# VectorE's Newton step of the previous unit, placed behind both sums of squares and two rotary products of its slot

## The reference

```python
def l2norm(t):
    return t / jnp.maximum(jnp.linalg.norm(t, axis=-1, keepdims=True), 1e-12)

q = l2norm(q) * qs
k = l2norm(k) * ksc
q = q * cos * scale + rotate_half(q) * sin * scale
k = k * cos * inv + rotate_half(k) * sin * inv
# local_attention: each window attends to itself and the window before
sim = jnp.where(mask, -max, einsum(q, k) * 8.0)
out = einsum(softmax(sim), v)
x = attn_layer(shift_tokens(x), ...) + x
x = ffn_layer(shift_tokens(x), ...) + x
```

## Time and profile before

| what | value |
|---|---|
| device time, median of 3 | 4176.0 us (4174.39 to 4178.6) |
| the profiled execution | 4172.81 us |
| its span, first to last instruction | 4171.0 us |
| PE busy | 3756.9 us (90%) |
| DVE busy | 3466.0 us (83%) |
| ACT busy | 3183.2 us (76%) |
| POOL busy | 2641.4 us (63%) |

### The profile page before, as it was taken

The page is one execution under the profiler, slowest core; times in us unless marked ns, Lnnn a source line. Parts: engine busy times, 40 slices in busy tenths (PEclk is TensorE's granted clock), DMA queues, the critical chain, the costliest instruction groups (busy, mean ns, idle before and its releaser), DMA issues. The chain is left out here.

```text
span 4171.0 us, 167237 instructions
## 1 busy us (share of the span) xinstructions
PE 3756.9 (90%) x66080; PEld 2932.9 (70%) x66080; DVE 3466.0 (83%) x6851; ACT 3183.2 (76%) x10379; POOL 2641.4 (63%) x2482
## 2 busy tenths in 40 slices
PE   8958969999999999999995877999999999999996
PEld 7937947777777777777773546777777777777773
DVE  2242249999999999999984869999999999999994
ACT  4434438888888888888882666888888888888884
POOL 0000027777777777778761647787777877777771
PEclk9978979999999999999997898999999999999997
DMA  1000013333333343333330003333333333333331
GB/s 39 19 1 24 19 50 109 117 102 118 96 109 116 102 121 95 108 116 104 118 91 8 1 22 99 116 101 119 102 104 116 104 117 105 102 119 100 107 118 34
DMA packets 547031, 361.36 MB, mean 87 GB/s; under 512 B 32321, under 2 KB 532817, under 8 KB 546001
## 3 DMA queue, kind: packets, MB, share of 16 engines
q1 hardware_dynamic: 546256, 350.66, 28.1%
HBM read 248.59 MB, written 101.97 MB: 84 GB/s over the span
## 5 line engine op out<-in xcount | busy, mean ns | idle before, releaser
L1278 POOL TENSOR_TENSOR lt_t<-lt_t 128x512 f32<-128x512 f32 x768 | 973.7, 1289 | 567.1 <-DVE lt_t L1112 567.1
L1014 ACT ACTIVATE lt_pb<-lt_pb,lt_mx 128x64 f32<-128x64 f32 x3072 | 1023.4, 345 | 0.0
L1284 POOL TENSOR_TENSOR lt_t<-lt_t,lt_rn 128x512 f32<-128x512 f32 x768 | 811.0, 1077 | 117.3 <-DVE lt_rn L1140 116.0
L49 PE MATMUL ps<-lt_wh,lt_xh 128*128 128x512 f32 (+1 forms) x1536 | 581.7, 379 | 150.1 <-DVE lt_t L1112 88.8
L1014 ACT ACTIVATION_READ_ACCUMULATOR lt_pb<-lt_pb,lt_mx 128x1 f32 x3072 | 609.3, 198 | 0.0
L996 ACT ACTIVATE lt_qkT<-ps 128x512 f32<-128x512 f32 x768 | 459.1, 598 | 196.8 <-PE ps L816 196.8
L1123 DVE TENSOR_REDUCE lt_ss<-lt_sq 128x8 f32<-128x512 f32 x768 | 518.9, 676 | 14.1 <-ACT lt_sq L991 9.9
L1112 DVE TENSOR_TENSOR lt_t<-ps,lt_tab 128x512 f32<-128x512 f32 x768 | 523.1, 682 | 2.9
L1118 DVE TENSOR_TENSOR lt_t<-ps,lt_tab 128x512 f32<-128x512 f32 x768 | 522.1, 680 | 1.9 <-PE ps L816 0.6
L51 PE MATMUL ps<-lt_wh,lt_xl 128*128 128x512 f32 (+1 forms) x1536 | 523.2, 341 | 0.0
L50 PE MATMUL ps<-lt_wl,lt_xh 128*128 128x512 f32 (+1 forms) x1536 | 522.8, 340 | 0.0
(11 more groups left out here) (213 smaller groups left out, 7653.0 us busy)
## 6 DMA issues: line engine op xcount, KB each, us to landing
lt_vw<-v_scratch SPq DMA_DIRECT2D x768, 256.0 KB, 3.8
v_scratch<-lt_vv SPq DMA_DIRECT2D x384, 256.0 KB, 2.1
lt_wraw<-in_lt_wqkv SPq DMA_DIRECT2D x56, 384.0 KB, 5.8
moe_w<-in_moe_w SPq DMA_DIRECT2D x32, 256.0 KB, 2.8
lt_wo<-in_lt_wo SPq DMA_DIRECT2D x48, 128.0 KB, 3.8
lt_w<-in_lt_w SPq DMA_DIRECT2D x12, 341.0 KB, 4.4
lt_w<-in_lt_w SPq DMA_DIRECT2D x12, 192.0 KB, 4.0
lt_gl<-in_lt_qs SPq DMA_DIRECT2D x2, 768.0 KB, 7.5
```

What stands on the lines that cost most here:

```text
L49: nc.tensor.matmul(out, lh, rh, start=start, stop=False)
L1014: ins = nc.scalar.activation(p, p, ACT.Exp, bias=mx[:, par, c:c + 1], accum_out=sm[:, par, c:c + 1])
L1278: nc.gpsimd.tensor_tensor(o, o, t2[:, t, :], ALU.add).then_inc(padd[t], 1)
L1284: nc.gpsimd.tensor_tensor(o, o, rn[:, u[1] % 2, 8 * t:8 * t + 8].unsqueeze(2).to_broadcast([P, 8, DH]), ALU.mult).then_inc(qkd[t], 1)
```

## The change

In VectorE's slot the Newton step of u1 moves from its place behind `maxima` to the place between the second sine product and `floor` of u0. GpSimd's, TensorE's and ScalarE's orders stay.

```diff
                     if u3:
                         maxima(u3)
-                    if u1:
-                        newton(u1)
                     c = chunk(L, s, 17)
                     if c:
                         product(c, 0)
...
                         cosine(u0, 0)
                         lengths(u0, 1)
                         sine(u0, 1)
+                    if u1:
+                        newton(u1)
+                    if u0:
                         floor(u0)
                     if u5 and u5[1] % GJ == GJ - 1:
                         update_x(u5)
```

## The result

Median of the runs side by side: 4129.09 us after (4126.63 to 4134.39) against 4175.19 before (4174.05 to 4178.6), a ratio of 0.989 [0.9873, 0.9907]: 46 us faster. The forecast was 20 us. The profiled execution took 4131.38 us, its span 4129.6.

What follows compares the result with a forecast made beforehand. VectorE and TensorE were both taken to be at their limit, VectorE partly blocked by GpSimd. Ordinary pairs +8, slot-15 pairs -8, layer boundaries -20 gave -20 us: median 4156, own range 4135 to 4175, wide range 4100 to 4210.

Steps and rivals of the forecast that it cites:

- What bounded the kernel: VectorE and TensorE both at their limit; Newton operations held up by GpSimd, 0.76 us a slot, 293 us in all.
- What comes later: rn, hence GpSimd's 5.87 us chain to the weights' transposes: new waits in slots without feed-forward work ahead.
- The other signs: Waits before take_values, lengths, product; GpSimd several hundred us on rn, little on rotary products; VectorE's share down 9 points.
- What goes: TensorE's waits on VectorE in slots 3, 4 and 5 of a pair: about 0.8 us gone.
- the forecast of an ordinary pair: Later transposes and gelus +0.2+0.41+0.14+0.37, vanished waits -0.8: +0.3 us on 64.41, +8 us over 24 pairs.
- The pair with slot 15: Loses more to blocked Newton steps before the change: 0.8 us shorter, ten times, -8 us.
- The pair at a layer's boundary: Newton steps stood behind GpSimd's four 1.8 us operations: -1.8 us, eleven times, -20 us.
- The floor: Directly behind rn, done before GpSimd's scaling starts: cost 0; if it lost, up to 1.0 us of the slot.
- the third rival: Floor operation blocked by GpSimd's scaling, rotary products 1.05 us later: +100 to 120 us, 4270; chance 0.06.
- The feed-forward normalisation: In slot 7, moves up to GpSimd's weight normalisation; both passes can be blocked: 0 to 0.3 us a pair.
- The second rival: GpSimd's chain to the weights' transposes longer, or VectorE's passes later: slots 0, 2, 3, 4 pay, 4200; chance 0.22.
- the first (4100): GpSimd's chain stays hidden, TensorE becomes the bound and its waits on VectorE all go: about 4100; chance 0.20.

Runs made afterwards that it cites:

- e4: Kernel before, old order, its three Newton operations replaced by one-input reductions of the same shape, refinement left out: 4046.44 us, ratio 0.9688.
- e1: Changed kernel with the Newton step behind three passes instead of four, the second sine product between it and the floor: 4143.73 us, ratio 0.9923.
- e2: Changed kernel with the Newton step behind two passes, leaving two passes between rn and the floor: 4251.56 us, ratio 1.0188.
- e8: Changed kernel with the Newton step behind three passes and the floor directly behind rn, ahead of the second sine product: 4100.83 us, ratio 0.9817.
- e5: Changed kernel, new order, its three Newton operations replaced by one-input reductions, refinement left out: 4157.16 us, ratio 0.9951 to before.
- e9: Kernel before, old order, Newton step and floor written as one-input reductions over pairs, nothing left out, four operations instead of three: 4078.76 us, ratio 0.9763.
- e7: Kernel before, old order, GpSimd's normalisation of the weights on 4 of 8 groups only: 4080.24 us, ratio 0.9769.

## Why the prediction was right in kind and short in size

**What bounded the kernel.** Right: the excess in two Newton operations was time spent waiting for GpSimd, and part of it was on the path. e4 prices that part at 131 us, where 293 us were held up. Of the rest, much lay where TensorE sets the pace: slot 7 keeps 9.04 us without the block. The Trainium skill's rule that weight loads measure TensorE's headroom better than matmuls (Perfetto Trace Analysis, Identifying the Most-Contended Engine) would have given 3880. No run here bears it out: with the block gone, e4 stands at 4046 with weight loads busy for 72% of its span. In slot 7 of an ordinary pair of e4 matmuls fill all of the 9.04 us, weight loads 6.62.

**What comes later.** Right in its instants, term by term. The chain from rn to the transposes: 5.87 us forecast, 5.90 measured. The transposes behind their projection: in slot 0 4.18 forecast and 4.18 measured (2936.97 to 2941.15); in slot 2 4.58 and 4.55; in slot 3 3.99 and 3.98; in slot 4 3.94 and 3.80. Slot 1 is 0.31 longer, forecast 0.2. Those are the instants. Their cost to an ordinary pair was forecast as 1.12 us and measured, after against e4, as about 1.6; slot 3 makes the difference, 0.5 instead of 0.14, as below. The other signs came too: VectorE waits 111 us in front of take_values (39 before), 125 in front of product (45) and 36 in front of lengths (10), and GpSimd 656 for rn and 13 for the rotary products. VectorE's share of the stretch fell by 6 points, not 9.

**What goes.** Here the step failed: "TensorE's waits on VectorE that go, in slots 3, 4 and 5: about 0.8 us". Before against e4 gives about 1.7 us: 0.6 in slot 3, 0.7 to 0.9 in slot 4, 0.17 in slot 7, the rest below 0.1. I had taken the 0.8 from the sum of a row of waits. A row of waits counts the idle time behind the modelled end of the operation before, and matmuls overlap. TensorE before, in slots 3 and 4 of the pair of the earlier trace rows:

```profile
3117.92 0.39 PE L50 MATMUL ps<-lt_wl,lt_xh 128*128 128x512 f32 x1
3118.15 0.39 PE L51 MATMUL ps<-lt_wh,lt_xl 128*128 128x512 f32 x1
3118.70 0.63 PE L816 MATMUL ps<-ident,lt_t 128*128 128x128 f32 x4 [0.16 <-DVE lt_vv L1163]
...
3130.65 0.28 PE L51 MATMUL ps<-lt_wh,lt_xl 128*128 128x256 f32 x1
3131.15 1.10 PE L895 MATMUL ps<-X,avg 128*128 128x512 f32 x2 [0.22 <-DVE X L1169]
```

Matmuls of 128x512 start 0.23 us apart (3117.92 to 3118.15), though each is shown with 0.39. The transpose at 3118.70 follows by 0.55: it is 0.32 late, and the row says 0.16. The matmul at 3131.15 comes 0.50 behind one of 128x256, which start 0.12 apart in this place: 0.38 late, and the row says 0.22. So a wait that is shown is about 0.16 us too small here, and one that is shorter than that isn't shown. Besides, these two wait for take_values and for update_x, which I hadn't counted, as I looked for waits on the rotary products alone. In e4 the transposes of slot 3 follow their projection by 3.47 instead of 3.85. My 3.99 was right as an instant, and yet I booked it as 0.14 above a base that the block itself had raised.

That step alone made the forecast of an ordinary pair wrong in sign, +0.3 where -0.16 was measured: the credit was 0.9 too small and the cost 0.45 too small, so the two errors partly hid each other. The other two credits were too small as well. The pair with slot 15: 0.8 forecast, 1.4 measured (65.6 to 64.2; its slot 7 from 9.95 to 9.03). The pair at a layer's boundary: 1.8 forecast, 2.3 measured (68.82 to 66.48). There the wait of 2.07 us at 3034.79 is gone, and the transposes of slot 3 wait 1.75 us where they waited 0.62.

**The sum, redone for a layer** of 32 slots. Before it lasted 263.21 us (2804.25 to 3067.46), in e4 253.15 (2783.55 to 3036.70), after 259.22 (2784.49 to 3043.71). So unblocking is worth 10.1 us a layer, the late rn costs 6.1, and 4.0 remain: two ordinary pairs at 0.16, 1.4 from slot 15's and 2.3 from the boundary. My terms for the same layer: 2 x 0.3 - 0.8 - 1.8 = -2.0. Twelve layers make 48 and 24 us, against 46 measured and 20 forecast.

**The floor and the rivals.** The floor was right at nothing: 227 ns. It starts 0.09 us after rn, the scaling 0.26, and e1 and e2 show that this place is what keeps it free; with passes in between, the third rival happens. The feed-forward normalisation does meet GpSimd now (948 ns on average for its first pass, 684 before), but slot 7 of an ordinary pair, 9.04 us against 9.17 to 9.21, shows no cost: the low end of the 0 to 0.3 forecast. The second rival (a longer chain, 4200) didn't come about, since the chain was the one forecast. Neither did the first (4100): GpSimd's chain isn't hidden behind four passes. With one pass less, as in e8, the waits for it are halved, and the time is 4101. The measured 4129 lies inside the wide range of 4100 to 4210 and misses the narrower one of 4135 to 4175, which went with the sum.

## What to carry to other kernels

Compare the mean duration of a small operation with its shortest one: where they differ, it waits inside itself, and another place, with operations of its kind directly behind one another, or a form with a single input takes that wait away. Follow what you delay to the next engine that has a queue behind it, step by step to the instant at which somebody waits; those instants came out here to some hundredths of a microsecond, 0.14 at worst. The worth of a stall that goes is read from the starts of successive instructions against a slot without it, or from a run in which it can't happen, never from a sum of waits.

## What the runs showed of the hardware

**Who is held up.** VectorE's operations with two inputs in SBUF on 16 columns took 0.16 to 0.18 us at their shortest, about 0.97 behind GpSimd's 1.04 us normalisation and up to 1.75 behind its 1.8 us operations on new weights. Reductions with one input took 0.15 to 0.19 in every instance of e4, e5 and e9, at the same places beside the same work. The rotary passes, which read PSUM, took 0.67 to 0.69 in every instance. The Trainium skill (SBUF — State Buffer, SBUF: two separate sides) says that VectorE's operations with two SBUF inputs, and those in a two-port mode, and GpSimd's operations share a port pair, which the first to start keeps for its whole instruction. The trace agrees, and e7 shows it by size: 0.43 us less of GpSimd took 0.49 from the two operations behind it. GpSimd pays as well: 1.49 us for its normalisation where VectorE's 128x512 pass came first, 1.04 otherwise.

**How little decides.** VectorE 0.32 us ahead of GpSimd or 0.07 behind it made 1.2 us of difference to the same two operations. In e5, where the shorter work ahead turned the order round, the kernel was slower (4157 against 4129); that the turned order is the reason is not shown.

**The place of a step** has no simple slope: at 0 passes 4175 us, at 2 4252, at 3 4144, or 4101 with the floor next to rn, at 4 4129, at 6 4511.
